# Scalar comparisons in a graph layer's edge loop, and another order of sums in its node update

## What is computed

```python
row, col = (ei[0], ei[1])
filt = jax.nn.silu(rbf @ Wf1 + bf1) @ Wf2 + bf2
msg = x[col] * filt
agg = jax.ops.segment_sum(msg, row, num_segments=x.shape[0])
h = jax.nn.silu(agg @ Wu1 + bu1) @ Wu2 + bu2
mean = jnp.mean(h, axis=0)
var = jnp.mean(jnp.square(h - mean), axis=0)
bn = gamma * (h - mean) * jax.lax.rsqrt(var + BN_EPS) + beta
```

## Time and profile before

| what | us |
|---|---|
| median of 3 runs (2083.26 to 2089.93) | 2088.68 |
| the profiled execution, own time | 2100.86 |
| its span, first to last instruction | 2099.1 |
| busy: PE / DVE / POOL / ACT | 1882.4 / 1501.5 / 1443.0 / 1332.9 |
| edge loop, first to last indirect DMA | 165.45 to 1647.09 |
| node update, up to the last statistics | 1652.3 to 1767.4 |

### The profile page before, as it was taken

One profiled execution on the slowest core, in us unless ns is written; L12 is line 12 of the kernel. 1 busy time (PEld: TensorE's weight loads), 2 busy tenths in 40 slices (PEclk: granted clock), 3 DMA queues, 4 the chain that ended last, 5 costly groups with the idle time before them and its releaser, 6 DMA issues. The chain is left out here.

```text
span 2099.1 us, 38406 instructions
## 1 busy us (share of the span) xinstructions
PE 1882.4 (90%) x9844; PEld 1548.4 (74%) x9844; DVE 1501.5 (72%) x3453; ACT 1332.9 (63%) x2412; POOL 1443.0 (69%) x997
## 2 busy tenths in 40 slices
PE   5989999999989998998899889999997298799998
PEld 3667888787778787777777777877786276577778
DVE  6967877777777767776777677776775287788846
ACT  4547776776677667666766576667664067577733
POOL 2216888888888888888888888888888564355600
PEclk9999999999999999999999999999999599699979
DMA  9888888988988798878988898888897793000002
GB/s 370 319 299 169 162 159 166 173 159 143 172 165 160 137 172 168 157 140 162 176 146 154 156 177 142 157 159 167 150 158 115 202 322 120 12 0 0 0 31 103
DMA packets 288979, 325.41 MB, mean 155 GB/s; under 512 B 30118, under 2 KB 251721, under 8 KB 288688
## 3 DMA queue, kind: packets, MB, share of 16 engines
q0 software_dynamic: 112896, 102.81, 40.0%
q1 hardware_dynamic: 172576, 217.21, 32.4%
q10 hardware_dynamic: 3280, 2.83, 0.5%
HBM read 167.64 MB, written 154.97 MB: 154 GB/s over the span
## 5 line engine op out<-in xcount | busy, mean ns | idle before, releaser
L994 POOL DMA_INDIRECT sums<-x_rows,out_idx x784 | 1226.3, 1564 | 288.3 <-issue 207.2
L1048 PE MATMUL bank<-wf,x_rows 128*128 128x256 f32 x3136 | 800.5, 384 | 0.0
L1048 PEld LDWEIGHTS bank<-wf,x_rows 128*128 128x128 f32 x3136 | 545.2, 192 | 54.3
L1172 ACT ACTIVATE x_rows<-bank,bf 128x512 f32<-128x512 f32 x392 | 270.4, 690 | 279.8 <-PE bank L1026 277.1
L1268 DVE TENSOR_TENSOR msg_low<-bank,msg_high 128x512 fp32r<-128x512 f32 x392 | 271.3, 692 | 162.0 <-ACT msg_high L1192 162.0
L1299 DVE TENSOR_TENSOR bank<-bank,x_rows 128x512 f32<-128x512 f32 x392 | 272.7, 696 | 119.4 <-PE bank L1048 114.5
L1046 PE MATMUL bank<-gnn_bf_halves,ones 128*128 128x256 f32 x784 | 296.5, 378 | 0.0
L1192 ACT ACTIVATE msg_high<-bank 128x512 fp32r<-128x512 f32 x392 | 234.3, 598 | 88.5 <-DVE bank L1299 85.8
L1180 ACT ACTIVATE x_rows<-pair 128x516 f32<-128x516 f32 x392 | 234.1, 597 | 63.7 <-DMA sums<-x_rows,out_idx 62.9
L1199 ACT ACTIVATE x_rows<-bank 128x512 f32<-128x512 f32 x392 | 235.2, 600 | 36.9 <-PE bank L1036 33.4
L1036 PE MATMUL bank<-window,spread 128*128 128x256 f32 x784 | 193.2, 328 | 58.2 <-DVE spread L1263 37.2
(11 more groups left out here) (331 smaller groups left out, 2740.2 us busy)
## 6 DMA issues: line engine op xcount, KB each, us to landing
window<-xn_halves SPq DMA_DIRECT2D x392, 128.0 KB, 4.2
sums<-gate SPq DMA_DIRECT2D x32, 800.0 KB, 10.8
x_rows<-id_rows SPq DMA_DIRECT2D x98, 256.0 KB, 5.0
x_rows<-attr_rows SPq DMA_DIRECT2D x98, 256.0 KB, 4.7
xn_halves<-xn_halves SPq DMA_DIRECT2D x7, 1792.0 KB, 7.3
x_rows<-id_rows SPq DMA_DIRECT2D x98, 128.0 KB
sums<-x_rows,out_idx POOLq DMA_INDIRECT x784
res<-sums SPq DMA_DIRECT2D x24, 512.0 KB, 7.7
```

The source lines that it names most:

```text
L994: nc.gpsimd.indirect_dma_start(g.sums_dram[k], bass.IndirectOffsetOnAxis(ap=out_idx[:, ET * c + t:ET * c + t + 1], axis=0), summed[c % 2][ ...
L1048: mm = T.matmul(out, hidT[:, j // 2, f, ds((2 * (j % 2) + t) * P, P)], g.wf2[:, f, :], start=False, stop=f == CB - 1)
L1172: A.activation(hidT[:, h, f, :], hps[:], ACT.Silu, bias=g.bf1[:, f:f + 1]).then_inc(hid_ready, 1)
```

## The change

Three edits. `spread` and `same` are made by a comparison with a per-partition scalar instead of one with a broadcast tensor; for `same` that takes an instruction for each tile, so two for each pair. In the node update DVE does low_sums(u+1) ahead of gather_sums(u+2). For units 0 and 1 DVE adds tables 2 and 3 as well; POOL starts with unit 2.

```diff
@@ indicate
-                V.tensor_tensor(spread[:, j % 2, :], id_row[:, p, ds(2 * EC + j * PC, PC)],
-                                g.half_f[:].to_broadcast([P, PC]), ALU.is_equal).then_inc(spread_ready, 1)
+                V.tensor_scalar(spread[:, j % 2, :], id_row[:, p, ds(2 * EC + j * PC, PC)], g.half_f[:, 0:1], None,
+                                ALU.is_equal).then_inc(spread_ready, 1)
@@ equal
-                V.tensor_tensor(same[:, p, 2 * j:2 * j + 2, :], id_row[:, p, ds(2 * j * PC, 2 * PC)].bitcast(I16).rearrange("p (t n) -> p t n", n=P),
-                                g.src_f[:, ds(c * ET + 2 * j, 2)].unsqueeze(2).to_broadcast([P, 2, P]),
-                                ALU.is_equal).then_inc(same_ready, 1)
+                for t in (2 * j, 2 * j + 1):
+                    op = V.tensor_scalar(same[:, p, t, :], id_row[:, p, ds(t * PC, PC)].bitcast(I16),
+                                         g.src_f[:, ds(c * ET + t, 1)], None, ALU.is_equal)
+                op.then_inc(same_ready, 1)
@@ POOL in update_nodes
-            for u in range(3):
-                late_sums(u)
+            late_sums(2)
@@ gather_sums
-                dve.wait_ge(two_ready, u + 1)
-                dve.wait_ge(late_ready, u + 1)
+                if u < 2:
+                    d = part[u % SETS][:, 3, 0:len(unit_tiles(u)), :]
+                    V.tensor_tensor(c, c, d, ALU.add).then_inc(two_ready, 1)
+                    dve.wait_ge(two_ready, 2 * u + 2)
+                else:
+                    dve.wait_ge(two_ready, u + 3)
+                    dve.wait_ge(late_ready, u - 1)
                 V.tensor_tensor(a, a, c, ALU.add).then_inc(agg_ready, 1)
@@ DVE's rounds in update_nodes
             for u in range(UNITS):
+                if u + 1 < UNITS:
+                    low_sums(u + 1)
                 if u + 2 < UNITS:
                     gather_sums(u + 2)
-                if u + 1 < UNITS:
-                    low_sums(u + 1)
```

## The result

The changed kernel took 2074.64 us (median of 6 runs, 2071.75 to 2081.07) against 2089.3 for the kernel before beside it: ratio 0.9928, 95% interval 0.9903 to 0.9953. Timed a second time it took 2076.73 us (9 runs), ratio 0.9936 (0.9910 to 0.9962). So it is faster, by 14.7 and 14.4 us; the forecast of 2086, no difference that can be told, was not what came, though the range held it.

The account below looks back on a forecast made before the run. POOL's issue of indirect DMAs was taken to bound the edge loop. Terms -3 + 0 on the profiled 2100.9 gave 2097.9, and the median lies 12.2 lower: 2086 us against 2088.68, range 2073 to 2101.

Parts of the forecast that it names:

- What bounds the loop: Edge loop: POOL issues its indirect DMAs almost without pause, so only changes to POOL's own row move the loop.
- Edit 1: Edge loop: scalar comparisons for `spread` and `same` shorten the indirect DMAs they delay; taken as -3 us.
- two ends: Edge loop, DMA lengthening by both comparisons: -6.6 us if POOL gets between the two of `same`, +3.9 if they block together.
- The rule from the earlier trace: Edge loop: a comparison in flight over an indirect DMA's start lengthens it by the comparison's end after that start, less 0.13 us.
- Edit 2: Node update: the new order and adds start `hidden` of unit 1 5.4 us earlier, but later waits use that up; taken as 0.
- the lead: Node update: the 5.4 us by which `hidden` of unit 1 starts earlier; forecast to be used up by later units.
- The term of 0: Node update: its net effect on the time, taken between -5.4 us (early start kept) and +11 us.
- the hand schedule: Node update units set out by hand with the measured durations: the early start falls from 5.4 to 2.4 us by unit 6.
- The ports come free: Edge loop: scalar comparisons never hold POOL up, -9.9 us, 2079; 2073 with the node update's early start kept; chance 0.28.
- A wait for the sum: Node update, PE's `turn_sums`: waits of 0.8 to 1.95 us for each of 11 units; +11, 2100 us; chance 0.14.
- Held in mid-flight: Edge loop: scalar comparisons stop POOL's indirect DMAs after their start; +54 us, 2143; chance 0.04.
- Nothing changes: Whole kernel: comparisons take as long and the order only moves waits about; 2088.7 us; chance 0.08.

Follow-up runs that it names:

- both splits: The changed kernel with L1253's subtraction cut into four pieces and `spread`'s comparison into two; 2068.41 us (ratio 0.9898), and again 2074.22 us (0.9922).

## Why the prediction came out as it did

**What bounds the loop: right.** The prediction's reading, POOL's own row and nothing else, holds in every kernel here: DVE's busy time rose by 28 us, and DVE's row numbers ended no more than 1.9 us of POOL's gaps in either profile of the change (5.2 at most, in a kernel with both splits); the DMAs still start 0.30 after the one before.

**Edit 1: the step that failed is the -3.** The prediction had two ends, -6.6 where POOL gets in between the two of `same`, +3.9 where both act as a block of 0.50, and took a value between. The rows decide for the first end. Over four kernels with both comparisons scalar and four with both as before, their cost went from 9.7 to 2.4 us, -7.3. It should have been taken whole: the reason that stood there ("should not wait for an instruction that has not begun") named the mechanism, and no row spoke for the block. The rule from the earlier trace rows that the ends were worked out with needs a limit: it holds for the comparisons and L1253, not for `message` and `msg_low`. The ends, made of comparisons alone, don't change by it.

Its other flaw is the method: new durations were put at the old starts. POOL's DMAs and DVE's list run against each other with periods of about 1.84 and 3.78, so a DMA that starts earlier meets the next thing. In the same two fours L1253, untouched, rose from 6.2 to 9.3, and the gaps fell from 20.2 to 18.1. The loop's mean went from 1479.6 to 1473.3: -6.3 = -7.3 + 3.1 - 2.1, good to about 3 us by the scatter of the four. The sum agrees with the -6.6 by errors that cancel, which is luck.

Durations: `same` as predicted, 0.28 alone and 0.47 for a pair (0.50 predicted); `spread` 0.35 in most rows (0.35 predicted), 402 ns in the mean, since 97 of 392 last 0.45 or more. Those begin 0.46 to 1.13 after a DMA's start; the tensor comparisons of the kernel before, begun there, took at most 0.43. So a scalar form does wait inside a DMA, by up to 0.34 (0.28 predicted), and a tensor form of these comparisons doesn't. DVE's longer pair was free, as said.

**Edit 2: the gain right, the account of its loss not, the sum nearly.** Unit 1 started 5.3 us earlier (5.4 predicted), the waits moved to `turn_sums` for DVE's adds, and the lead was used up: six profiles with both edits of the update and the new order throughout took 113.6 in the mean (110.3 to 117.6), four with neither 114.6. The term of 0 measured -1.0 by the profiles and -2.0 +- 2.2 by the times. That it is *the order of later rounds* that loses the lead, as the hand schedule had it, fell with the kernel that has it in the first round only. What does lose it stays open; POOL's and DVE's adds, which the orders share, are the candidate, and that was not tried.

**The rivals.** *The ports come free* comes nearest in time (2079, or 2073 with the lead kept), but not in its mechanism: scalar comparisons do still hold a DMA's start, only briefly, and the lead was not kept. That 2074.64 lies near its 2073 owes some 4 us to the clock (below), which is luck; at the same clock the change stands at about 2079, and the range holds that too. *A wait for the sum* is there and worth less than the lead: not 0.8 to 1.95 at each of 11 units, but 0.25, 0.27 and the 1.92 above at three (the 3.15 above is unit 1's, which waited 2.51 before). *Held in mid-flight* fell: 150 DMAs show nothing. The Trainium skill, "SBUF — State Buffer", section "Who interferes with whom", has the later of the two blocked for the whole of the other. That is not this rival, as the prediction had it, for in the rival the earlier one waits. Nor is it what the rows show: a scalar comparison that begins inside a DMA waits 0.34 at most, not to the DMA's end, and the runs decide. *Nothing changes* is out.

**What the sum left out.** Loop -6.3 and update -1.0 make -7.3, good to about 3 us. At the same granted clock the change gives -10.5 +- 2.0. Comparisons alone and update alone add up to -8.4 +- 3.2, and the 2.1 by which the change gives more is inside its uncertainty of 3.5. So some us may have no place in the views used here, or none. The remaining 4 us of the -14.7 go with the mean granted clock of whole runs: of 96 runs of before 35 had 0.961 or less, of the change's 15 none. Either edit alone didn't do that (6 and 4 of 12); the later kernels with both edits had 5 of 43. The late fall in the unchanged last part is the likely place, since "rest" is 312 to 316 us in the profiles without it and 320 to 326 in those with it. But two profiles with it had means of 0.963 and 0.965, and a run without a profile doesn't show where its clock was low. The prediction had no term for the clock, and why low means are rarer with both edits stays open.

## What to carry to other kernels

Where an engine's queue is the bound, look for what is in flight on the engine that shares with it when its next instruction starts, check in the rows that it holds that start up (`message`, just as long, doesn't), and cut it: the queue then waits only for the piece that has begun, even if the cut work takes longer in all (four pieces 0.91 us against 0.69 in one). Expect less than such a count promises, since the instructions that start earlier meet other neighbours: over four profiles each, the loop kept 6.3 of 7.3 us for the comparisons and 5.6 of 7.2 for L1253, and at the same clock the time got only 2.7 of the latter; four profiles of one loop tell more than one. Before two profiles are subtracted, compare their granted clock stretch by stretch, also where the code is the same.

## What the runs showed of the hardware that was not expected

- An indirect DMA that starts among several comparisons, or pieces of L1253, waits for those that have begun and not for the next. A scalar pair ending 0.29 after the start cost 0.00; four tensor pieces ending 0.66 after it cost 0.12, one piece ending 0.62 after it 0.49.
- Not every instruction holds a start up: `message` and `msg_low` (0.69, one operand in `bank`) were in flight over 241 starts in the changed kernel and cost 0.2 us in all.
- A scalar comparison that begins 0.46 to 1.13 into an indirect DMA lasts up to 0.69 instead of 0.35; a tensor comparison that begins there takes 0.43 at most, against 0.42 in the mean.
- Changing one DVE line moved another's collisions: `same`, unchanged, went from 52 contacts to 90 when only `spread` was shortened.
- A pause of PE of 1.9 us was followed by a fall to 1.2 GHz for 3.4 us in one profile and by none in another. Over the 226 runs the time follows the mean granted clock, 1.37 us for 0.001, which alone spreads the runs of one kernel over some 18 us (before: 0.956 to 0.969, and 2079.8 to 2104.4 us in all).
